# Layer 1's experts in an eight-part transformer kernel: token lists made by products on TensorE, rows gathered and answers scattered tile by tile

## The chip, the cores and the metric

The kernel runs on one core of a Trainium2 chip. The metric is the device time of one execution in microseconds. The engines of the core run their own instruction streams and meet through semaphores: PE (TensorE, matrix products), DVE (VectorE), ACT (ScalarE), POOL (GpSimd) and SP (SyncE), which here only issues transfers. POOL can also issue transfers whose rows are picked by a list of indices (indirect DMA).

## The reference, cut to what matters

Four layers, each a cross-attention followed by a token-mixing part and a feed-forward part. `B * S` is 2 * 512 = 1024 tokens of width 128. The change concerns the feed-forward part of layer 1 alone, where each token goes to the one expert of eight with the largest logit:

```
logits = xf @ Wg.T
idx = jnp.argmax(logits, axis=-1)
for e in range(E):                      # E = 8
    m = (idx == e)[:, None]
    h = relu(xf @ W1[e] + b1[e])        # 128 -> 512
    out = out + m * (h @ W2[e] + b2[e]) # 512 -> 128
```

## The kernel before

The 1024 tokens lie in on-chip memory as eight tiles of 128 (NT = 8); `r_res` holds them, token t * 128 + p in partition p. The kernel sorts the tokens by expert so that each expert multiplies only its own. Each expert's queue is padded to whole tiles of 128 rows, so 8 + 8 - 1 = 15 tiles (`TILES1`) always suffice, each with one expert.

`places1` on DVE (line 1794) and PE (line 2439) works out where each token goes: a mask of the chosen expert, a product with a triangle of ones to count the tokens ahead, the first tile of each expert, and from these `slot_i`, the row of each token in the sorted order (line 1820). Then `tile_e`, the expert of each tile (line 1827). After that DVE runs `centre_weights` (lines 1365 to 1369), which prepares layer 2's weights and has nothing to do with the experts, and `add_biases` (line 1862).

The rows take a path through HBM. POOL (`queues1`, line 890) scatters the eight token tiles into `queued`, one indirect DMA each, `sent` counting them. SP loads tile by tile from `queued` into four buffers `D["xin"]` (`tokens`, line 722) and that tile's expert weights, 514 KB, into four buffers `W0` (`weights`, line 717). It stores each tile's answer into `answers` (line 738). When all 15 are stored, POOL gathers the eight token tiles back out of `answers` with eight indirect DMAs (line 901), and DVE adds them to `r_res` (line 1856).

SP's loop over the tiles is in one order: for tile j it waits for the turned tile j and loads tokens j + 4, waits for output j and loads weights j + 4, waits for answer j and stores it. So tokens j + 5 are issued behind the wait for answer j.

PE's order for the tiles is written out by hand too (line 2446 on). `turned(j)` transposes the tile's tokens, `hidden(j)` multiplies by W1, `output(j)` by W2:

```
turned(0)
turned(1)
hidden(0)
for j in range(TILES1):
    if j + 2 < TILES1:
        turned(j + 2)
    if j + 1 < TILES1:
        hidden(j + 1)
    output(j)
```

DVE copies each turned tile out (`features`, line 1835) and each answer (`answer`, line 1841) into one of four buffers `D["y"]`; ACT applies ReLU (line 1233). Behind the last answer PE runs `prep(2)`, layer 2's keys and values (lines 2033 to 2085), with ACT's copies of its results (lines 993 and 999). DVE, behind the sum of line 1856, runs two layer norms; then layer 2's attention begins with PE's line 2100.

Of the kernel before, what the change touches and what calls it, by code (L numbers as in the profile page):

```python
# [58 lines left out]
E0 = 16  # L59
SLOTS = E0 * CAPACITY  # L60
TILES1 = B * S // P + 8 - 1
assert CAPACITY == P
HS, DS = 16, 8

# [20 lines left out]
def queue_constants():  # L85

    e = np.arange(8)
    wide = lambda v: np.broadcast_to(np.asarray(v, np.float32).reshape(1, -1), (P, np.size(v)))
    return {
        "r_steps": wide(P * e),  # L90
        "r_ahead": wide(P * (e[None, :] < e[:, None])),
        "r_within": wide(e[None, :] <= e[:, None]),
        "r_tile": wide(np.arange(16)),
    }


# [81 lines left out]
    return np.concatenate([w1.reshape(8, 4, P, P).transpose(0, 2, 1, 3).reshape(8, P, 4 * P), w2], 2)  # L178


def program(nc, x, mask, packed, experts, rows, zeros, out, answers, queued, parts_q, parts_k, at):


    ctx = ExitStack()
    with ctx:
        def sb(name, shape, dt=F32):
            return ctx.enter_context(nc.sbuf_tensor(name, shape, dt))
# [28 lines left out]
        pool_pad = sb("pool_pad", [P, 8])  # L216
        n_sum = sb("n_sum", [P, 40])
        slot_i = sb("slot_i", [P, 16], I32)
        tile_e = sb("tile_e", [P, 16], I32)
        s1_now = sb("s1_now", [P, 2, 4])  # L220
        ident_bf = sb("ident_bf", [P, P], BF16)
        later_bf = sb("later_bf", [P, P], BF16)
# [63 lines left out]
        ranks, row_sums = D["xin"][:, 0:P], D["xin"][:, 2 * P:2 * P + 64]  # L286
        chosen = [D["back"][:, n * 1024:(n + 1) * 1024] for n in range(2)]
        W0 = [wexp[:, 0, :], wexp[:, 1, :], D["w"][:, 0:1028], D["w"][:, 1028:2056]]


        in_x, in_mask, stored, const_ok = sems("in_x in_mask stored const_ok")
# [326 lines left out]
        def _(sp):  # L618
# [88 lines left out]
            sp.dma_start(queued, zeros).then_inc(cleared, 16)  # L707
# [7 lines left out]
            def queues1():  # L715

                def weights(j):
                    e = sp.value_load(tile_e[0:1, j:j + 1], min_val=0, max_val=7)
                    src = experts[1].rearrange("e p n -> p e n")[:, bass.ds(e, 1), :]
                    sp.dma_start(W0[j % 4].unsqueeze(1), src).then_inc(w0_in[j % 4], 16)  # L720

                def tokens(j):
                    sp.dma_start(D["xin"][:, j % 4 * P:(j % 4 + 1) * P], queued[j * P:(j + 1) * P, :]).then_inc(q_in[j % 4], 16)

                sp.wait_ge(tiles_ok, 1)
                for j in range(4):
                    weights(j)
                sp.wait_ge(sent, 16 * NT)
                for j in range(4):
                    tokens(j)  # L730
                for j in range(TILES1):
                    if j + 4 < TILES1:
                        sp.wait_ge(d_T, AFTER0 + j + 1)
                        tokens(j + 4)
                        sp.wait_ge(d_O, AFTER0 + j + 1)
                        weights(j + 4)
                    sp.wait_ge(d_y, HELD0 + j + 1)
                    sp.dma_start(answers[j * P:(j + 1) * P, :], D["y"][:, j % 4 * P:(j % 4 + 1) * P]).then_inc(d_stored[j % 4], 16)

            queues1()  # L740
            for l in range(2, 4):
# [23 lines left out]
        def _(pool):  # L765
# [123 lines left out]

            def queues1():  # L890

                pool.wait_ge(cleared, 16)
                pool.wait_ge(m_xn, 2 + B)
                pool.wait_ge(slots_ok, 2)
                for t in range(NT):
                    pool.indirect_dma_start(queued, bass.IndirectOffsetOnAxis(ap=slot_i[:, t:t + 1], axis=0),
                                            r_res[:, t * P:(t + 1) * P], None).then_inc(sent, 16)
                for side in range(4):
                    pool.wait_ge(d_stored[side], STORED0 + 16 * len(range(side, TILES1, 4)))
                for t in range(NT):  # L900
                    pool.indirect_dma_start(D["back"][:, t * P:(t + 1) * P], None, answers,
                                            bass.IndirectOffsetOnAxis(ap=slot_i[:, t:t + 1], axis=0)).then_inc(d_back[t // TB], 16)

            def router_norm3():

# [387 lines left out]
        def _(dve):  # L1293
# [443 lines left out]
            def gating(l):  # L1737
# [53 lines left out]
                if l != 2:  # L1791
                    add_biases(l)

            def places1():
                n, E_ = NT * 8, 8
                shape = [P, NT, E_]
                t3 = lambda v: v[:, 0:n].rearrange("p (t e) -> p t e", e=E_)
                e8 = lambda v: v.rearrange("p (e k) -> p e k", k=8)
                square = [P, 8, 8]
                m, pre, ga = t3(M["m12"]), t3(M["pre"]), t3(M["ga"])  # L1800
                tiles_of, start = small[:, 0, 32:40], small[:, 0, 40:48]
                ended = small[:, 1, 32:40]
# [12 lines left out]
                step.then(dve.tensor_tensor(e8(M["mk"][:, 64:128]), e8(w("r_ahead")), each, ALU.mult))  # L1815
                step.then(dve.tensor_reduce(start, e8(M["mk"][:, 64:128]), AX_X, ALU.add))
                step.then(dve.tensor_tensor(ga, t3(bank(0, 0, n)), start.unsqueeze(1).broadcast_to(shape), ALU.add))
                step.then(dve.tensor_tensor(ga, ga, m, ALU.mult))
                step.then(dve.tensor_reduce(small[:, 0, 48:56], ga, AX_X, ALU.add))
                dve.tensor_scalar(slot_i[:, 0:NT], small[:, 0, 48:56], 1.0, None, ALU.subtract).then_inc(slots_ok, 1)  # L1820
                step.then(dve.tensor_tensor(e8(M["mk"][:, 128:192]), e8(w("r_within")), each, ALU.mult))
                step.then(dve.tensor_reduce(ended, e8(M["mk"][:, 128:192]), AX_X, ALU.add))
                past = M["pre"][:, P:2 * P].rearrange("p (j e) -> p j e", e=8)
                step.then(dve.tensor_tensor(past, ended.unsqueeze(1).broadcast_to([P, 16, 8]),
                                            w("r_tile").unsqueeze(2).broadcast_to([P, 16, 8]), ALU.is_le))
                step.then(dve.tensor_reduce(small[:, 1, 40:56], past, AX_X, ALU.add))
                dve.tensor_scalar(tile_e[:, 0:16], small[:, 1, 40:56], 7.0, None, ALU.min).then_inc(tiles_ok, 1)

            def experts1():

# [6 lines left out]
                def answer(j):  # L1837
                    dve.wait_ge(d_O, AFTER0 + j + 1)
                    if j >= 4:
                        dve.wait_ge(d_stored[j % 4], STORED0 + 16 * (j // 4))  # L1840
                    dve.tensor_copy(D["y"][:, j % 4 * P:(j % 4 + 1) * P], bank(4 + j % 2, 0, P)).then_inc(d_y, 1)

                places1()
                centre_weights()
                dve.wait_ge(sent, 16 * NT)
                add_biases(1)
                features(0)
                features(1)
# [3 lines left out]
                    answer(j)  # L1852
                for b in range(B):
                    r_ = r_res[:, b * S:(b + 1) * S]
                    dve.wait_ge(d_back[b], BACK0 + 16 * TB)
                    step.then(dve.tensor_tensor(r_, r_, D["back"][:, b * S:(b + 1) * S], ALU.add))

            def add_biases(l):
# [150 lines left out]
        def _(pe):  # L2009
# [429 lines left out]
            def places1():  # L2439
# [3 lines left out]
                mm(bank(0, 0, n), w("before"), M["m12"][:, 0:n], start=True, stop=True)  # L2443
                mm(bank(0, 0, n), w("ones"), M["pre"][:, 0:n], start=False, stop=True, skip_group_check=True).then_inc(g_loc, 1)

            def experts1():

                def turned(j):
# [23 lines left out]

                places1()
                turned_gates(1)
                biases(1)
                pe.wait_ge(slots_ok, 2)
                turned(0)
# [158 lines left out]
```

## Time and profile before

| | us |
|---|---|
| median of 3 runs | 1107.84 (1106.42 to 1111.03) |
| the profiled execution | 1109.69 |
| its span in the trace | 1107.9 |
| mean granted clock of PE | 0.876 |

The rows further down are in microseconds from the span's start. A row of the timeline gives the start, the busy time, engine, line, operation, written tile <- read tiles, shape and how many instructions are merged in it; in brackets, how long the engine sat idle before it and who released it. `arena` is the large work buffer that holds `xin`, `xe`, `h`, `y`, `back`, and two of the four weight buffers (`wexp` is the other two). PEclk is the granted clock of TensorE as a share of 2.4 GHz, so that 0.50 is 1.2 GHz.

### The profile page before, as it was taken

The numbers are of one execution on the slowest core, as the hardware profiler recorded it, in microseconds if no ns is written. First come the engines' busy times: TensorE is split into PE (matmuls) and PEld (weight loads), VectorE is DVE, ScalarE is ACT, GpSimd is POOL, SyncE is SP. The second block draws the span as 40 slices with busy tenths as digits, with TensorE's granted clock in tenths as the row PEclk, the third lists the DMA queues.
The fourth block names the chain that finished last, engine by engine and source line by source line (L and its number), as shares of the span: only waits on it lengthen the run. The fifth ranks groups of instructions, "written<-read, shape, count | busy, mean of one in ns | idle before, by whom it ended". The sixth has DMA issues, their size and how long they took to land. (4 is left out here: it accounts for less than half of the span.)

```text
span 1107.9 us, 14863 instructions
## 1 busy us (share of the span) xinstructions
PE 877.4 (79%) x5294; PEld 602.6 (54%) x5294; DVE 577.2 (52%) x1254; ACT 410.1 (37%) x763; POOL 239.3 (22%) x274
## 2 busy tenths in 40 slices
PE   6895989839974654675769688998799988789998
PEld 4673445429962533565359522232466676557776
DVE  5784435446456556117567577771454548522111
ACT  3340535633332200342433326666322234343443
POOL 0543301000043205115545413000000014210110
PEclk9996869959987965796889959999899989978999
DMA  7005230053510001650000224100011100001111
GB/s 319 1 20 124 77 85 24 2 226 88 169 41 8 1 0 47 184 152 15 1 1 2 83 60 130 45 2 1 7 38 43 52 1 1 1 0 31 34 36 35
DMA packets 36031, 60.47 MB, mean 55 GB/s; under 512 B 4016, under 2 KB 27504, under 8 KB 35568
## 3 DMA queue, kind: packets, MB, share of 16 engines
q1 hardware_dynamic: 34944, 57.54, 16.7%
q0 software_dynamic: 1024, 2.10, 0.7%
q8 instruction: 38, 0.62, 0.2%
q14 instruction: 25, 0.20, 0.1%
HBM read 50.06 MB, written 10.35 MB: 55 GB/s over the span
## 5 line engine op out<-in xcount | busy, mean ns | idle before, releaser
L1578 DVE TENSOR_REDUCE arena<-psum 128x2 f32<-128x1024 f32 (+3 forms) x128 | 127.1, 1020 | 81.5 <-PE psum L2250 49.9
L1091 ACT ACTIVATE arena<-psum 128x512 f32<-128x512 f32 (+3 forms) x256 | 115.9, 515 | 87.1 <-PE psum L2263 48.0
L2521 PE MATMUL psum<-xT_all,wexp 128*128 128x512 f32 x272 | 124.6, 603 | 0.9 <-ACT arena L1192 0.6
L2247 PE MATMUL psum<-arena 72*128 72x512 bf16 (+3 forms) x256 | 83.0, 396 | 24.6 <-DMA arena<-parts_q 11.8
L777 POOL TENSOR_TENSOR rstd<-var,held 128x8 f32<-128x8 f32 (+3 forms) x22 | 46.0, 2099 | 252.9 <-DVE var L1333 229.7
L2175 PE MATMUL psum<-values_out_all,arena 128*128 128x128 f32 x560 | 76.4, 284 | 26.6 <-ACT arena L1055 26.0
L852 POOL TENSOR_TENSOR arena<-arena,small 128x616 f32<-128x616 f32 x56 | 68.0, 1217 | 125.7 <-DVE small L1510 125.4
L1917 DVE SCALAR_TENSOR_TENSOR x_res<-psum,arena,x_res 128x128 f32<-128x128 f32 x136 | 38.3, 344 | 101.6 <-PE psum L2536 101.6
L2175 PEld LDWEIGHTS psum<-values_out_all,arena 128*128 128x128 f32 x560 | 67.2, 192 | 36.2 <-ACT arena L1055 35.0
L2260 PE MATMUL psum<-arena 75*128 75x512 bf16 (+3 forms) x256 | 76.2, 362 | 8.2 <-DMA arena<-arena 6.5
L1042 ACT ACTIVATE arena<-arena 128x616 f32<-128x616 f32 x56 | 40.2, 717 | 108.1 <-DVE arena L1506 108.1
L2521 PEld LDWEIGHTS psum<-xT_all,wexp 128*128 128x128 f32 x272 | 50.3, 195 | 53.5 <-issue 48.3
L2247 PEld LDWEIGHTS psum<-arena 72*128 72x128 bf16 x256 | 23.4, 106 | 88.5 <-DVE arena L1578 45.5
L1203 ACT ACTIVATE arena<-psum,wexp,s_now 128x512 f32<-128x512 f32 x64 | 48.2, 778 | 62.3 <-PE psum L2521 59.1
L2536 PEld LDWEIGHTS psum<-arena 128*128 128x128 f32 x512 | 62.2, 199 | 6.9 <-issue 6.9
L2536 PE MATMUL psum<-arena 128*128 128x128 f32 x512 | 62.4, 283 | 0.0
L2301 PE MATMUL psum<-arena 128*32 128x512 f32 (+3 forms) x512 | 61.1, 556 | 1.5 <-ACT arena L1104 1.5
L1502 DVE TENSOR_REDUCE small<-psum 128x8 f32<-128x616 f32 x56 | 44.0, 787 | 34.5 <-PE psum L2152 25.2
L2152 PE MATMUL psum<-keys_of_tokens,xT_all 128*128 128x512 f32 (+1 forms) x160 | 52.3, 453 | 3.9 <-ACT xT_all L962 2.2
L2260 PEld LDWEIGHTS psum<-arena 75*128 75x128 bf16 x256 | 25.8, 104 | 40.4 <-ACT arena L1091 15.1
L1055 ACT ACTIVATE arena<-psum 128x640 f32<-128x640 f32 x56 | 38.8, 692 | 24.0 <-PE psum L2166 24.0
L1506 DVE TENSOR_TENSOR arena<-psum,small 128x616 f32<-128x616 f32 x56 | 44.8, 799 | 1.9
(326 smaller groups left out, 1532.4 us busy)
## 6 DMA issues: line engine op xcount, KB each, us to landing
wexp<-experts SPq DMA_DIRECT2D x24, 514.0 KB, 3.7
arena<-experts SPq DMA_DIRECT2D x15, 514.0 KB, 3.7
parts_k<-wexp SPq DMA_DIRECT2D x12, 384.0 KB, 3.0
arena<-parts_k SPq DMA_DIRECT2D x48, 96.0 KB
arena<-parts_q SPq DMA_DIRECT2D x48, 96.0 KB
arena<-rows SPq DMA_DIRECT2D x8, 512.0 KB, 8.0
wexp<-experts SPq DMA_DIRECT2D x9, 384.0 KB, 3.1
held<-packed SPq DMA_DIRECT2D x1, 2375.0 KB, 15.8
```

The lines of the kernel that those rows point to most:

```text
L777: pool.tensor_tensor(dst, src, half[0:src.shape[0], 0:n], ALU.pow).then_inc(done, 1)
L852: pool.tensor_tensor(e, e, inv, ALU.mult).then_inc(e_mul, 1)
L1091: act.activation(p_self[:, n % 2, kt % 2, j, lo:S], bank(t_bank("keys", c, k), lo, S), ACT.Exp, scale=DS ** -0.5).then_inc(ut_ok, 1)
L1203: act.activation(hT[:, b, c * BANK:(c + 1) * BANK], bank(c, 0, BANK), func, **kw).then_inc(h_ok, 1)
L1578: dve.tensor_reduce(top[:, x % 2, qt, j:j + 2], src, AX_X, ALU.max, negate=True).then_inc(us_ok, 1)
L2152: last = mm(psum[:, first + lo:first + hi], tokens, rows[:, b, half, lo:hi], start=True, stop=True)
L2175: last = mm(bank(sum_bank(l, t), 0, P), PT3[l][:, n % 3, c * P:(c + 1) * P], VW[:, t // TB, half, c * P:(c + 1) * P], start=(half == 0 and ...
L2247: last = mm(bank(first + n, 0, W), q_ring[0:ROWS, x % 4, j + n, qt * P:(qt + 1) * P], k_ring[0:ROWS, x % 4, j + n, 0:W], start=True, stop= ...
L2260: last = mm(bank(first, lo, S), k_ring[0:ROWS + 3, x % 4, j, kt * P:(kt + 1) * P], q_ring[0:ROWS + 3, x % 4, j, lo:S], start=True, stop=True)
L2301: last = mm(psum[32 * j:32 * j + 32, 7 * BANK + lo:8 * BANK], v_wide[b][:, kt, 4 * g + j, :], p_self[:, n // 2 % 2, kt % 2, j, lo:S], star ...
L2521: mm(bank(c, 0, BANK), wexp[:, side, c * P:(c + 1) * P], xT_all[:, b * S:(b + 1) * S], start=True, stop=True).then_inc(h_ps, 1)
L2536: last = mm(bank(4 + b, t * P, (t + 1) * P), hT[:, b, c * BANK + t * P:c * BANK + (t + 1) * P], down, start=(c == 0), stop=(c == C - 1))
```

## The change

The list of tokens is made the other way round: for each of the tiles, which token stands in each row. DVE writes two 0/1-like operands in bf16 (`lane_of`, 128 x 8 x 128, and `place_of`, 128 x 8 x 2 x 24), PE multiplies them in eight products accumulated in one bank (`rows_of_tiles`), and DVE turns the sums into `row_i`, the token number of row p of tile j; a row that no token has gets a number of its own behind the 1024 tokens.

SP stores `r_res` once, in token order, into `tokens_in`. POOL gathers the rows of tile j out of `tokens_in` with the list (`fetch`) and scatters the answer of tile j into `sorted_out` at the same list (`deliver`): for j = 0 to 14 `deliver(j)`, then `fetch(j + 4)`. SP's loop keeps only the weights. When all 15 answers are delivered, SP loads the answers back in token order with two plain loads, one per batch. On PE, `rows_of_tiles` stands ahead of `biases(1)`. `tile_e` gets 24 columns in place of 16.

```diff
+                sp.wait_ge(m_xn, 2 + B)
+                sp.dma_start(tokens_in[0:B * S, :].rearrange("(t p) d -> p t d", p=P),
+                             r_res[:, :].rearrange("p (t d) -> p t d", d=P)).then_inc(sent, 16)
                 sp.wait_ge(tiles_ok, 1)
                 for j in range(4):
                     weights(j)
-                sp.wait_ge(sent, 16 * NT)
-                for j in range(4):
-                    tokens(j)
-                for j in range(TILES1):
-                    if j + 4 < TILES1:
-                        sp.wait_ge(d_T, AFTER0 + j + 1)
-                        tokens(j + 4)
-                        sp.wait_ge(d_O, AFTER0 + j + 1)
-                        weights(j + 4)
-                    sp.wait_ge(d_y, HELD0 + j + 1)
-                    sp.dma_start(answers[j * P:(j + 1) * P, :], D["y"][:, j % 4 * P:(j % 4 + 1) * P]).then_inc(d_stored[j % 4], 16)
+                for j in range(TILES1 - 4):
+                    sp.wait_ge(d_O, AFTER0 + j + 1)
+                    weights(j + 4)
+                for side in range(4):
+                    sp.wait_ge(d_back[side], BACK0 + 16 * len(range(side, TILES1, 4)))
+                for b in range(B):
+                    sp.dma_start(D["back"][:, b * S:(b + 1) * S].rearrange("p (t d) -> p t d", d=P),
+                                 sorted_out[b * S:(b + 1) * S, :].rearrange("(t p) d -> p t d", p=P)).then_inc(d_stored[b], 16)
...
+                def fetch(j):
+                    if j >= 4:
+                        pool.wait_ge(d_T, AFTER0 + j - 3)
+                    pool.indirect_dma_start(D["xin"][:, j % 4 * P:(j % 4 + 1) * P], None, tokens_in,
+                                            bass.IndirectOffsetOnAxis(ap=row_i[:, j:j + 1], axis=0)).then_inc(q_in[j % 4], 16)
+
+                def deliver(j):
+                    pool.wait_ge(d_y, HELD0 + j + 1)
+                    pool.indirect_dma_start(sorted_out, bass.IndirectOffsetOnAxis(ap=row_i[:, j:j + 1], axis=0),
+                                            D["y"][:, j % 4 * P:(j % 4 + 1) * P], None).then_inc(d_back[j % 4], 16)
...
                 pool.wait_ge(cleared, 16)
-                pool.wait_ge(m_xn, 2 + B)
+                pool.wait_ge(sent, 16)
                 pool.wait_ge(slots_ok, 2)
-                for t in range(NT):
-                    pool.indirect_dma_start(queued, bass.IndirectOffsetOnAxis(ap=slot_i[:, t:t + 1], axis=0),
-                                            r_res[:, t * P:(t + 1) * P], None).then_inc(sent, 16)
-                for side in range(4):
-                    pool.wait_ge(d_stored[side], STORED0 + 16 * len(range(side, TILES1, 4)))
-                for t in range(NT):
-                    pool.indirect_dma_start(D["back"][:, t * P:(t + 1) * P], None, answers,
-                                            bass.IndirectOffsetOnAxis(ap=slot_i[:, t:t + 1], axis=0)).then_inc(d_back[t // TB], 16)
+                for j in range(4):
+                    fetch(j)
+                for j in range(TILES1):
+                    deliver(j)
+                    if j + 4 < TILES1:
+                        fetch(j + 4)
...
+            def places_in_tiles(n):
+
+                at, first = Z["at"][:, 0:n], Z["first"][:, 0:n]
+                slot = small[:, 0, 48:48 + n]
+                whole, lane = slot_i[:, 0:n], lane_i[:, 0:n]
+                step.then(dve.tensor_scalar(whole, slot, 1.0, None, ALU.subtract))
+                step.then(dve.tensor_scalar(lane, whole, P - 1, None, ALU.bitwise_and))
+                step.then(dve.tensor_tensor(first, whole, lane, ALU.subtract))
+                step.then(dve.tensor_scalar(at, lane, 1.0, None, ALU.add))
+                wide_j = [P, n, 24]
+                which = place_of[:, 0:n]
+                step.then(dve.tensor_tensor(which[:, :, 1, :], first.unsqueeze(2).broadcast_to(wide_j),
+                                            w("r_first").unsqueeze(1).broadcast_to(wide_j), ALU.is_equal))
+                dve.tensor_scalar(which[:, :, 0, :], which[:, :, 1, :], w("r_lane"), None, ALU.mult)
+                step.then(dve.tensor_tensor(which[:, :, 1, :], which[:, :, 1, :],
+                                            w("r_block", 0, n).unsqueeze(2).broadcast_to(wide_j), ALU.mult))
+                dve.tensor_tensor(lane_of[:, 0:n, :], at.unsqueeze(2).broadcast_to([P, n, P]),
+                                  w("places").unsqueeze(1).broadcast_to([P, n, P]), ALU.is_equal).then_inc(g_m, 1)
...
-                dve.tensor_scalar(slot_i[:, 0:NT], small[:, 0, 48:56], 1.0, None, ALU.subtract).then_inc(slots_ok, 1)
+                places_in_tiles(NT)
+                dve.wait_ge(g_loc, 3)
+                off, row = Z["off"], Z["row"]
+                lanes, blocks = bank(1, 0, 24), bank(1, 24, 48)
+                step.then(dve.scalar_tensor_tensor(off, blocks, 0.0, w("r_unused"), ALU.is_equal, ALU.mult))
+                step.then(dve.tensor_scalar(row, blocks, float(P), -float(P), ALU.mult, ALU.add))
+                step.then(dve.tensor_tensor(row, row, lanes, ALU.add))
+                dve.tensor_tensor(row_i[:, 0:24], row, off, ALU.add).then_inc(slots_ok, 1)
...
                     if j >= 4:
-                        dve.wait_ge(d_stored[j % 4], STORED0 + 16 * (j // 4))
+                        dve.wait_ge(d_back[j % 4], BACK0 + 16 * (j // 4))
...
-                dve.wait_ge(sent, 16 * NT)
+                dve.wait_ge(sent, 16)
...
-                    dve.wait_ge(d_back[b], BACK0 + 16 * TB)
+                    dve.wait_ge(d_stored[b], STORED0 + 16)
...
+            def rows_of_tiles(n):
+
+                pe.wait_ge(g_m, 3)
+                for i in range(n):
+                    last = mm(bank(1, 0, 48), lane_of[:, i, :], place_of[:, i].rearrange("p k j -> p (k j)"),
+                              start=(i == 0), stop=(i == n - 1))
+                last.then_inc(g_loc, 1)
```

## Rows read from the trace of the kernel before

**Rows 1.** Busy time by stage: the tiles' loop, and what follows until the sum.

```profile
451.00:491.00 40.00, 33.20 (x255) 30.62 (x256) 8.38 (x30) 17.15 (x60) 0.00 (x0) 0.95 0.66 188
491.00:507.00 16.00, 12.84 (x61) 10.56 (x59) 1.50 (x3) 6.41 (x10) 7.63 (x8) 0.79 0.14 38
```

**Rows 2.** Timeline from the places to the first tile, DVE, PE, POOL and SP.

```profile
432.96 0.55 PEld L2443 LDWEIGHTS psum<-arena,held 128*128 128x128 f32 x2
...
435.95 0.17 DVE L1820 TENSOR_SCALAR slot_i<-small 128x8 int32<-128x8 f32 x1
...
436.54 0.29 DVE L1824 TENSOR_TENSOR arena<-small,held 128x128 f32<-128x128 f32 x1
...
436.96 1.07 POOL L896 DMA_INDIRECT queued<-r_res,slot_i  x1 [9.60 <-DVE slot_i L1820]
437.18 0.17 DVE L1827 TENSOR_SCALAR tile_e<-small 128x16 int32<-128x16 f32 x1
...
438.39 1.48 SPq L720 DMA_DIRECT2D wexp<-experts  x2
...
446.33 0.96 POOL L896 DMA_INDIRECT queued<-r_res,slot_i  x1 [0.30 <-issue]
...
448.59 1.22 DVE L1862 TENSOR_TENSOR r_res<-r_res,psum 128x1024 f32<-128x1024 f32 x1 [5.80 <-DMA queued<-r_res,slot_i]
...
450.99 0.72 DVE L1835 COPY arena<-psum 128x128 f32<-128x128 f32 x2 [1.17 <-PE psum L2452]
```

**Rows 3.** Timeline of the tiles' loop: answers 0, 1, 4 and 14, tokens 6.

```profile
456.04 0.29 DVE L1841 COPY arena<-psum 128x128 f32<-128x128 f32 x1 [2.03 <-PE psum L2469]
...
457.93 0.29 DVE L1841 COPY arena<-psum 128x128 f32<-128x128 f32 x1 [1.41 <-PE psum L2469]
...
459.76 0.43 SPq L723 DMA_DIRECT2D arena<-queued  x1
...
463.24 0.33 PE L2452 MATMUL psum<-held,arena 128*128 128x128 f32 x1 [0.43 <-DMA arena<-queued]
...
465.40 0.29 DVE L1841 COPY arena<-psum 128x128 f32<-128x128 f32 x1 [1.50 <-PE psum L2469]
...
490.25 0.29 DVE L1841 COPY arena<-psum 128x128 f32<-128x128 f32 x1 [1.29 <-PE psum L2469]
```

**Rows 4.** DMA issues: KB each, median us from issue to landing.

```profile
wexp<-experts SPq DMA_DIRECT2D x24, 514.0 KB, 3.7
...
arena<-queued SPq DMA_DIRECT2D x15, 64.0 KB, 3.4
...
out<-x_res SPq DMA_DIRECT2D x1, 512.0 KB, 3.2
...
arena<-answers,slot_i POOLq DMA_INDIRECT x24, 2.5
queued<-r_res,slot_i POOLq DMA_INDIRECT x8, 3.6
```

**Rows 5.** Timeline behind the last answer: gathers, sum, layer 2's first products.

```profile
494.65 0.99 POOL L901 DMA_INDIRECT arena<-answers,slot_i  x1 [47.36 <-DMA answers<-arena]
...
506.17 0.69 DVE L1856 TENSOR_TENSOR r_res<-r_res,arena 128x512 f32<-128x512 f32 x1 [4.48 <-DMA arena<-answers,slot_i]
...
511.76 0.70 ACT L999 ACTIVATE values_out_all<-psum 128x640 f32<-128x640 f32 x1 [0.26 <-PE psum L2085]
...
522.84 2.31 PE L2100 MATMUL psum<-held,arena 77*128 77x77 f32 x16 [11.12 <-DVE arena L1441]
```

**Rows 6.** Busy time and clock in and behind three idle spells of PE.

```profile
496.40:499.50 3.10, 0.00 (x0) 0.00 (x0) 0.00 (x0) 3.08 (x6) 2.41 (x3) 0.93 0.20 57
499.50:506.00 6.50, 6.46 (x27) 6.46 (x28) 0.71 (x1) 1.29 (x2) 3.78 (x4) 0.51 0.19 50
558.50:560.80 2.30, 0.00 (x1) 0.00 (x0) 2.23 (x3) 1.20 (x1) 1.79 (x2) 0.93 0.00 0
355.35:357.40 2.05, 0.00 (x0) 0.00 (x0) 2.02 (x4) 1.31 (x2) 0.83 (x2) 1.00 0.00 0
```

More of the change, by code:

```diff
@@ L61 @@
 TILES1 = B * S // P + 8 - 1
+ROWS_OUT = B * S + TILES1 * P
 assert CAPACITY == P
@@ L92, in queue_constants @@
         "r_within": wide(e[None, :] <= e[:, None]),
-        "r_tile": wide(np.arange(16)),
+        "r_tile": wide(np.arange(24)),
+        "r_first": wide(P * np.arange(24)),
+        "r_block": wide(np.arange(1, 17)),
+        "r_lane": np.arange(P, dtype=np.float32).reshape(-1, 1),
+        "r_unused": B * S + P + np.arange(24 * P, dtype=np.float32).reshape(24, P).T,
     }
@@ L178, in row_layout, with program @@
     return np.concatenate([w1.reshape(8, 4, P, P).transpose(0, 2, 1, 3).reshape(8, P, 4 * P), w2], 2)
-def program(nc, x, mask, packed, experts, rows, zeros, out, answers, queued, parts_q, parts_k, at):
+def program(nc, x, mask, packed, experts, rows, zeros, out, answers, sorted_out, tokens_in, parts_q, parts_k, at):
     ctx = ExitStack()
@@ L218, in program @@
         slot_i = sb("slot_i", [P, 16], I32)
-        tile_e = sb("tile_e", [P, 16], I32)
+        tile_e = sb("tile_e", [P, 24], I32)
+        row_i = sb("row_i", [P, 24], I32)
+        lane_i = sb("lane_i", [P, 16], I32)
         s1_now = sb("s1_now", [P, 2, 4])
@@ L288, in program @@
         W0 = [wexp[:, 0, :], wexp[:, 1, :], D["w"][:, 0:1028], D["w"][:, 1028:2056]]
+        Z = take(dict(lane=1024, which=2 * 24 * 8, off=24, row=24, at=16, first=16))
+        lane_of = Z["lane"].bitcast(BF16).rearrange("p (n c) -> p n c", c=P)
+        place_of = Z["which"].bitcast(BF16).rearrange("p (n k j) -> p n k j", k=2, j=24)
         in_x, in_mask, stored, const_ok = sems("in_x in_mask stored const_ok")
@@ L706, in _ @@
                 sp.dma_start(rows3[:, e, :], rows[e]).then_inc(n_in, 16)
-            sp.dma_start(queued, zeros).then_inc(cleared, 16)
+            sp.dma_start(tokens_in[B * S:ROWS_OUT, :], zeros).then_inc(cleared, 16)
             with sp.Fori(0, E0 // 4 - 1) as i:
@@ L720, in weights @@
                     sp.dma_start(W0[j % 4].unsqueeze(1), src).then_inc(w0_in[j % 4], 16)
-                def tokens(j):
-                    sp.dma_start(D["xin"][:, j % 4 * P:(j % 4 + 1) * P], queued[j * P:(j + 1) * P, :]).then_inc(q_in[j % 4], 16)
+                sp.wait_ge(m_xn, 2 + B)
+                sp.dma_start(tokens_in[0:B * S, :].rearrange("(t p) d -> p t d", p=P),
+                             r_res[:, :].rearrange("p (t d) -> p t d", d=P)).then_inc(sent, 16)
                 sp.wait_ge(tiles_ok, 1)
@@ L1819, in places1 @@
                 step.then(dve.tensor_reduce(small[:, 0, 48:56], ga, AX_X, ALU.add))
-                dve.tensor_scalar(slot_i[:, 0:NT], small[:, 0, 48:56], 1.0, None, ALU.subtract).then_inc(slots_ok, 1)
+                places_in_tiles(NT)
[6 more added lines that the diff above has]
+                dve.tensor_tensor(row_i[:, 0:24], row, off, ALU.add).then_inc(slots_ok, 1)
                 step.then(dve.tensor_tensor(e8(M["mk"][:, 128:192]), e8(w("r_within")), each, ALU.mult))
                 step.then(dve.tensor_reduce(ended, e8(M["mk"][:, 128:192]), AX_X, ALU.add))
[L1823 to L1827, printed above, removed]
+                past = M["h"][:, 2048:2240].rearrange("p (j e) -> p j e", e=8)
+                step.then(dve.tensor_tensor(past, ended.unsqueeze(1).broadcast_to([P, 24, 8]),
+                                            w("r_tile").unsqueeze(2).broadcast_to([P, 24, 8]), ALU.is_le))
+                step.then(dve.tensor_reduce(small[:, 2, 0:24], past, AX_X, ALU.add))
+                dve.tensor_scalar(tile_e[:, 0:24], small[:, 2, 0:24], 7.0, None, ALU.min).then_inc(tiles_ok, 1)
             def experts1():
@@ L2474, in experts1 @@
                 turned_gates(1)
+                rows_of_tiles(NT)
                 biases(1)
@@ L2628 @@
     answers = nc.dram_tensor("answers", (SLOTS, P), F32, kind="Internal").ap()
-    queued = nc.dram_tensor("queued", (TILES1 * P, P), F32, kind="Internal").ap()
+    sorted_out = nc.dram_tensor("sorted_out", (ROWS_OUT, P), F32, kind="Internal").ap()
+    tokens_in = nc.dram_tensor("tokens_in", (ROWS_OUT, P), F32, kind="Internal").ap()
     parts_q = nc.dram_tensor("parts_q", (2, B, 3 * P, S), BF16, kind="Internal").ap()
@@ L2632 @@
     program(nc, ap["x"], ap["mask"], ap["packed"], [ap[f"experts{l}"] for l in range(4)], ap["rows"], ap["zeros"], out, answers,
-            queued, parts_q, parts_k, at)
+            sorted_out, tokens_in, parts_q, parts_k, at)
     r = run_bass_kernel_spmd(nc, [arrays], core_ids=[0])
```

## The prediction

> **What bounds the kernel now.** I read the busy time by stage first [rows 1]. In the tiles' loop, 451 to 491, PE is busy for 33.2 of 40 us at a clock of 0.95: near its limit, not at it. From 491 to 507 PE and ACT work on layer 2's keys, and DVE, which layer 1 needs, is busy for 1.5 of 16 us: a wait. So three pieces count: from the places to the first tile, the loop, and from the last answer to the sum.
>
> The timeline ahead of the loop [rows 2] shows DVE's list of places at 435.95, POOL's eight scatters from 436.96 to 446.33 and DVE idle for 5.80 us until they have landed at 448.59. The first features are copied at 450.99, because the tokens are loaded only then. What is to be seen: the scatters end last here, and `centre_weights`, from the end of 437.18 to 5.80 us before 448.59, some 5.4 us, costs nothing.
>
> In the loop [rows 3] answers 0 and 14 start 34.21 us apart, 2.44 a tile. Follow one round: answer 1 ends at 458.22, SP stores it and issues tokens 6 at 459.76, they land 3.4 to 3.5 us later [rows 3, 4], PE turns them at 463.24, and answer 4 ends at 465.69. This wait comes around once for **three** tiles, 7.47 us, since tokens j + 5 stand behind the store of answer j, and PE turns tile j + 5 ahead of output j + 3. From the turn to the end of that answer are 2.45 us.
>
> Behind the loop [rows 5]: answer 14 ends at 490.54, the gathers start at 494.65, the last half of the sum starts at 506.17, 15.63 us after the answer.
>
> **The change part by part: the start.** DVE gets four small instructions at 0.20 each (0.17 for 128x8 [rows 2] and the gap to the next), 0.80; three over 192 elements, put at 0.39 each with the gap: 0.29 for 128 elements [rows 2], 0.07 more for 64 more, 1.17; one over 1024 elements, 1.22 as the one at 448.59. That is 3.2, to 439.15. PE's eight bf16 products don't occur here: the nearest rows are fp32 products at the same low clock, 0.27 a load [rows 2], which is the upper bound, 2.2 us for eight; half of it is the lower, 1.1. As bf16 makes one pass, I take 1.3, to 440.45. Four small DVE instructions more, 0.9: `row_i` is ready at 441.3, where `slot_i` was at 436.12. The fetches start as late after it as the scatters did, 0.84, so at 442.15, and land 2.5 later [rows 4]: nothing waits for them. `tile_e` comes 5.3 later, at 442.65, the weights are issued 1.04 behind it as before [rows 2], at 443.7, and land by 447.5 (3.7 [rows 4]). The cover of `centre_weights` is gone: DVE ends it at 448.1, `add_biases` at 449.35, and copies the first features then, 1.65 earlier than at 450.99. So DVE's own work ends last, and eight scatters buy **1.65 us**; with the bounds of the products 0.7 to 1.9. Answer 0 ends at 454.7. The store of `r_res` (512 KB, 3.2 us for the same size [rows 4]) is issued before 432.96, where PE already counts tokens, and is over long before 442; the four weight loads behind it on SP's queue are not held. PE's biases run a few us later, ahead of 448.
>
> **The loop.** The tokens now wait on POOL: `deliver(j)` for answer j, behind it `fetch(j + 4)`. PE turns tile j + 4 ahead of output j + 2. The round closes after **two** tiles, not three. Its parts: from DVE's end to an indirect DMA's start 0.84 [rows 2]; the scatter's issue, (446.33 - 436.96) / 7 = 1.34 at worst and 1.27 where DVE is quiet (0.96 and the 0.30 of issue), I take 1.27; the gather's landing; 2.45 from the turn to the answer. The landing is 2.5 alone, 3.6 beside four weight loads (median of the scatters [rows 4]), 2.2 at the least (446.33 to 448.55). The weights of tile j + 4 are issued some 0.4 after answer j and the gather 2.1, mostly behind them, so 2.8. A round is 0.84 + 1.27 + 2.8 + 2.45 = 7.36, that is 3.68 a tile. Turned tiles 4 to 14 let answers 2 to 12 go, six rounds, 44.2; answers 13 and 14 need none, and end 3.9 later as before. The loop lasts 48.1 in place of 34.2: **+13.9**. POOL itself needs 2.54 a tile, above the 2.44 of before, so that even with no latency this loop isn't shorter.
>
> The Trainium skill (DMA: Bandwidth & Descriptors, Anatomy of one DMA, the gpsimd path) gives an indirect DMA about 2.0 us plus its bytes over 436 GB/s, 2.15 for 64 KB. By it a round would be 6.7 and the sum 3.9 lower; the rows of the gathers, 2.5, stand nearer to this case.
>
> **The clock.** In a round PE works for twice some 2.1 us and then sits idle for about as long as the gather takes, 2.5 to 3.6. Before, it waited 0.43 in the row shown [rows 3]. In this trace the clock fell in a spell of 3.1 and in one of 2.3, and not in one of 2.05 [rows 6]; behind the first it stayed at 0.51 for 6.5 us of work. At 1.2 GHz the products of a turn, a hidden and an output take about twice as long, and 2.45 becomes 4.0. When it falls, PE works almost without a break and it rises again; I take half of the 1.55 in each of six rounds: **+4.5**, bounds 0 and 9.3.
>
> **The end.** Answer 14, 0.84 to the last scatter, 2.5 until it lands (2.2 to 3.6), SP's load at once; 256 KB in 2.8, between the 2.5 of 64 KB gathered and the 3.2 of 512 KB [rows 4]; 0.5 for the second load. The last half of the sum starts 6.9 us after answer 14, where it was 15.63: **-8.7** (bounds -9.5 and -7). Eight gathers in a row become two loads. Behind it layer 2's first product (522.84) stood 16.67 after the sum and ACT's last copy of prep (511.76 to 512.46) 21.9 after answer 14 [rows 5]; now the first would be due 23.6 after answer 14: prep stays hidden, by 1.7 us.
>
> **Sum.** -1.65 + 13.9 + 4.5 - 8.7 = +8.05 us. The profiled execution of before took 1109.69, with 1.8 around its span of 1107.9; it would be 1117.7. It lies 1.85 above the median, so that the median goes to 1115.9. The measurement tells 0.5%, 5.5 us, from no change.
>
> **Rivals.**
> *The clock holds.* PE's idle spells stay between the 2.05 and 2.3 us of the rows, or the work on either side keeps it up. Then +3.5, 1111.4: no measurable change. For it speaks that the spell with 2.05 passed; against it that every gather in the trace takes 2.5.
> *The clock falls in every round.* For it speaks the spell of 2.3 us. All of 1.55 is paid six times: +12.8, 1120.6. The Trainium skill (TensorE: Matmul & The Clock Gate, HAM oscillation) describes this case, short bursts of products with a wait for a DMA between them, and has every burst start cold; by it this rival, not the half, is the sum. The rows show both kinds of spell, so it gets no more than its share below.
> *The gather is as slow as the scatters beside the weights*, 3.6 or more: 0.8 in six rounds, +4.8 on the sum, 1120.7. Against it: four loads stood in line there, here one.
> *Faster.* POOL's wake decides: between two indirect DMAs in a row it takes 0.30 [rows 2], not 0.84. If `deliver`, the only thing POOL waits to do, starts so soon, and the gather lands in 2.2, a round is 0.30 + 1.27 + 2.2 + 2.45 = 6.2 and the loop 41.2. With a clock that holds the sum is -1.65 + 7.0 - 9.5 = -4.2, 1103.7. A round has to be below 6.0 us for it to be measurable; the one wake from a wait in the trace, 0.84, speaks against it.
>
> **How the numbers follow.** Half-cold clock, round about 7.4 (+5.5 to +11): 0.40. Clock holds (0 to +5.5): 0.33. Cold in each round, or the slow gather (+11 to +17): 0.20. Faster by over 5.5: 0.07. The first and third are slower by over 0.5%, but for the lower edge of the first, 0.04: slower 0.56, same 0.37, faster 0.07. Range: 1106.5 (the clock holds, gather 2.2, a short wake in part) to 1123 (cold in each round and 3.0 of landing); about a tenth is left out on either side.
>
> **What will show it.** `row_i` near 441.3 and features 0 near 449.4, with DVE busy without a gap from 436 on, not waiting for a DMA. Answers in pairs, two every 7.4 us, PE waiting for the gathers of `fetch` in front of each pair, answer 14 near 507 to 508. PEclk in the loop well under the 0.95 of before. From answer 14 to the last half of the sum about 7. Wrong would make it: answers evenly under 3 us apart (the round isn't the bound), a PEclk of 1.00 there, or the weights of `tile_e` landing later than DVE's 448.

## The result

| | before | after |
|---|---|---|
| median | 1108.74 us of 4 runs (1106.42 to 1111.03) | 1123.48 us of 4 runs (1120.02 to 1124.14) |
| the profiled execution, its span | 1109.69, 1107.9 | 1123.24, 1121.4 |

The ratio is 1.0145, with a 95% interval of 1.0118 to 1.0172: **slower by 1.45%**, some 15 us, where 0.7% and 8 us were forecast. The time lies 0.5 us above the range that was given.

Start of layer 1's experts after the change, from the timeline (start, busy time, engine, line, what, how many; in brackets the idle time before it). These answer to [rows 2].

```profile
438.75 0.50 PE L2492 MATMUL psum<-arena 128*128 128x48 bf16 x8 [3.20 <-DVE arena L1826]
...
439.94 0.18 DVE L1862 TENSOR_TENSOR row_i<-arena 128x24 int32<-128x24 f32 x1
...
440.92 1.04 POOL L902 DMA_INDIRECT arena<-tokens_in,row_i  x1 [13.82 <-DVE row_i L1862]
...
446.96 1.22 DVE L1904 TENSOR_TENSOR r_res<-r_res,psum 128x1024 f32<-128x1024 f32 x1
448.21 0.49 DVE L1877 COPY arena<-psum 128x128 f32<-128x128 f32 x2
```

The list is ready at 440.12; DVE has no gap from there to the first features at 448.21, and waits for no DMA, where before it stood idle for 5.80 us. The first features come 2.78 earlier than the 450.99 of before. But answer 0 ends at 454.65, only 1.68 earlier: from the features to the answer, 6.44 in place of 5.34, PE works at half clock for longer (0.50 until 454.6; before it was 1.00 from 455.0). Of both gains 0.27 isn't the change's: in this execution `slot_i` itself starts at 435.68, before at 435.95.

One round of the loop after the change, answers 6 to 8, from the timelines of DVE, PE, POOL and SP. It answers to [rows 3].

```profile
482.37 0.29 DVE L1883 COPY arena<-psum 128x128 f32<-128x128 f32 x1 [2.94 <-PE psum L2519]
...
482.94 0.99 POOL L907 DMA_INDIRECT sorted_out<-arena,row_i  x1 [5.10 <-DVE arena L1883]
483.07 2.25 SPq L730 DMA_DIRECT2D arena<-experts  x2
...
484.23 0.97 POOL L902 DMA_INDIRECT arena<-tokens_in,row_i  x1 [0.30 <-issue]
...
484.27 0.29 DVE L1883 COPY arena<-psum 128x128 f32<-128x128 f32 x1 [1.41 <-PE psum L2519]
...
488.69 0.39 PE L2502 MATMUL psum<-held,arena 128*128 128x128 f32 x1 [4.46 <-DMA arena<-tokens_in,row_i]
488.87 1.94 PE L2510 MATMUL psum<-arena,wexp 128*128 128x128 f32 x8
...
492.48 0.29 DVE L1883 COPY arena<-psum 128x128 f32<-128x128 f32 x1 [3.07 <-PE psum L2519]
```

To be seen: answers in pairs, 482.37 and 484.27, the next pair from 492.48. Answer 6 ends at 482.66; 0.28 later POOL issues its scatter, 1.29 later the gather of tile 10, which lands 4.46 after its issue; PE, idle for those 4.46 us, turns it at 488.69; answer 8 ends 4.08 later, at 492.77. SP's two weight loads of the pair are issued at 483.07 and 484.99, on either side of that gather. A round of two tiles, 10.11 us. The six rounds take 9.17, 8.91, 9.93, 10.11, 10.44 and 7.93, and answers 0 to 14 span 60.67 us where it was 34.21.

Busy time by stretch (length, then PE, PEld, DVE, ACT and POOL busy with their counts, granted clock, DMA share, GB/s): the loop from answer 0 to 14, the end until the last half of the sum, and one idle spell of PE with the stretch behind it.

```profile
454.65:515.32 60.67, 36.25 (x227) 34.73 (x226) 7.04 (x26) 14.86 (x52) 24.50 (x25) 0.83 0.43 122
515.32:521.65 6.33, 5.73 (x24) 3.30 (x24) 0.70 (x2) 2.39 (x3) 0.97 (x1) 1.00 0.34 104
484.40:488.60 4.20, 0.00 (x0) 0.00 (x0) 0.16 (x1) 0.20 (x1) 2.76 (x3) 1.00 0.83 254
488.60:491.60 3.00, 2.91 (x14) 2.91 (x15) 0.29 (x1) 0.67 (x3) 0.00 (x0) 0.54 0.16 56
```

The clock is 1.00 while PE is idle, 0.54 for the first tile behind it, and rises during the second (0.89 from 491.60 to 494.40). DMA is 0.83 busy in the very stretch in which the gather is awaited. The last half of the sum starts 6.33 us after answer 14, where it was 15.63.

Issues of two of the new transfers in the DMA view (KB, median from issue to landing), which answer to [rows 4]:

```profile
arena<-sorted_out SPq DMA_DIRECT2D x2, 256.0 KB, 2.9
...
arena<-tokens_in,row_i POOLq DMA_INDIRECT x15, 3.7
```

Where the time went: answer 0 earlier by 1.68, the loop longer by 26.46, the end shorter by 9.30, which puts the last half of the sum 15.48 later (521.65 against 506.17). The addition into `x_res` behind it is 15.50 later (532.19 against 516.69); layer 2's first sum of attention is 13.88 later (600.84 against 586.96), and so it stays until the end, 13.5. Layer 2's start gives the 1.6 back at a higher clock: in the 5.5 us from 555.0 the granted clock is 1.00, where in the same work of before, from 539.5, it was 0.69, and four instructions of 512 columns there take 1.89 in place of 3.10.

### The profile page after: what moved, and what is told of

It is laid out like the page before. It is cut to its first block and busy times, and to the rows that moved or that the text cites. A ratio compares the mean times of both kernels' runs of the same rounds, so it can differ in the third digit from the quotient of the medians.

```text
span 1121.4 us, 14872 instructions
## 1 busy us (share of the span) xinstructions
PE 887.1 (79%) x5297; PEld 612.7 (55%) x5302; DVE 580.7 (52%) x1265; ACT 410.2 (37%) x763; POOL 253.4 (23%) x288
```

## The experiments

Each is the changed kernel with the edit shown; "..." stands for lines left out. Loop means from the end of answer 0 to the end of answer 14; landing is read for the six gathers that let a round go (tiles 4, 6, ... 14), from issue to PE's turn. The runs with few or half of the weights, without scatters and with extra products are one execution each, so their times tell only large differences; the argument rests on the rows of their traces.

### Why the gather takes 4.1 us: the weights, or the scatter ahead of it

The six landings in the changed kernel were 4.25, 3.59, 4.32, 4.46, 4.89 and 3.25, mean 4.13, against 2.5 in [rows 4]. First, from tile 4 on, only 64 of the 1028 columns of the weights are loaded:

```diff
                     sp.wait_ge(d_O, AFTER0 + j + 1)
-                    weights(j + 4)
+                    weights(j + 4, 964)      # columns 964 to 1027 alone
```

> The changed kernel, but from tile 4 on only the last 64 of the 1028 weight columns of each tile are loaded (32 KB in place of 514 KB), so those tiles are multiplied with weights left over from other tiles. It asks why a gather in the loop takes about 4.1 us from issue to landing (six rounds: 3.2 to 4.9) and not the 2.5 of before. Theory A, the gather shares the DMA engines with two weight loads of 514 KB that SP issues in the same moment: the landing falls to 2.5 to 2.8, a round of two tiles from 9.4 to about 7.5, answer 0 to answer 14 from 60.7 to about 49 us, the span by about 11. Theory B, the gather stands behind the scatter of the answer that POOL issued 1.3 us ahead of it on the same queue: the landing stays near 4, the span stays within 2 us.

Timeline of a round, answers 2 to 4:

```profile
459.63 0.29 DVE L1883 COPY arena<-psum 128x128 f32<-128x128 f32 x1 [1.50 <-PE psum L2519]
...
461.50 0.97 POOL L902 DMA_INDIRECT arena<-tokens_in,row_i  x1 [0.30 <-issue]
...
464.08 0.33 PE L2502 MATMUL psum<-held,arena 128*128 128x128 f32 x1 [1.83 <-DMA arena<-tokens_in,row_i]
...
466.24 0.29 DVE L1883 COPY arena<-psum 128x128 f32<-128x128 f32 x1 [1.50 <-PE psum L2519]
```

Here 459.63 is answer 2 and 466.24 answer 4. The gather of tile 6 lands 2.58 after its issue; the six lie between 2.54 and 2.64, mean 2.59 (of the five gathers of odd tiles four do too, within 0.03, and that of tile 9 took 3.73, for which the trace shows no reason). A round is 6.6 us, the loop 43.04, the clock in it 1.00, the time 1104.7 of one run, 18.8 under the changed kernel. Theory A holds, and by more than was expected of it, because with the short waits the clock doesn't fall either. The edit takes away both, so the loop's 17.6 us are not the weights' price alone; the landing, 1.5 a round, is read by itself. The round is the sum of its parts: 0.28 + 1.30 + 2.58 + 2.45 = 6.61.

The counter-test takes the scatters out. SP stores each answer as a plain block in tile order, so that the answers don't come back in token order:

```diff
+                    sp.wait_ge(d_y, HELD0 + j + 1)
+                    sp.dma_start(sorted_out[j * P:(j + 1) * P, :], D["y"][:, j % 4 * P:(j % 4 + 1) * P]).then_inc(d_stored[j % 4], 16)
...
-                for j in range(TILES1):
-                    deliver(j)
-                    if j + 4 < TILES1:
-                        fetch(j + 4)
+                for j in range(TILES1 - 4):
+                    pool.wait_ge(d_y, HELD0 + j + 1)
+                    fetch(j + 4)
```

> The changed kernel with the scatters taken out: SP stores each answer as one plain block in tile order (so the answers are not brought into token order), POOL still waits for answer j and then gathers tile j + 4. Theory A (weights beside the gather): the landing stays near 4, a round is 0.28 + 4.1 + 3.7 = 8.1, the loop about 52. Theory B (behind the scatter): the landing falls to 2.5 to 2.8, the round to about 6.7, the loop about 44.

The six landings were 4.11, 4.27, 4.10, 5.70, 4.46 and 4.35, no shorter than with the scatters; the loop took 50.58, with the 1.3 us of issue gone from each round and a clock of 0.90 (1112.29 us). So a scatter ahead on POOL's queue isn't what makes the gather late. SP's stores move the same 64 KB in its place, so this run doesn't say what those bytes cost beside the gather.

Between the two, half of the weights' columns (the edit of the first run with column 514):

> The changed kernel, but from tile 4 on only the last 514 of the 1028 weight columns are loaded (257 KB in place of 514 KB; the rest is left over from other tiles). The landing of the gathers in the loop was 2.6 us with 32 KB and 4.1 with 514 KB. Theory, it is the bytes that stand in the DMA engines ahead of and beside the gather: something between, 3.2 to 3.5, a round of about 7.3 to 7.8 with the clock holding for part of it, loop 47 to 50. Rival, any pair of full-width loads costs the whole 1.5 us however short: landing near 4, loop above 55.

The landings were 3.03, 2.63, 2.85, 2.60, 3.19 and 2.50, mean 2.80 (1109.9 us): half of the bytes cost 0.2 us and the other half 1.3. The expectation of 3.2 to 3.5 missed. The loop of 48.10 came out as expected for another reason: the clock was 0.86, so that turn to answer took 3.1 in place of 2.45. In these three runs the delay isn't proportional to the bytes; how it grows was not measured further.

### What the clock costs

Products that nobody reads are put in front of the awaited turn, so that PE does not sit idle:

```diff
+                pe.wait_ge(b2_ok, 2)
                 for j in range(TILES1):
+                    if j >= 2 and j % 2 == 0 and j + 2 < TILES1:
+                        for k in range(7):                       # 4 in the second run
+                            mm(bank(7, 0, BANK), w("ones"), xT_all[:, 0:BANK], start=True, stop=True)
                     if j + 2 < TILES1:
                         turned(j + 2)
```

> The changed kernel with seven extra products of 512 columns (3.0 us at full clock) in PE's stream ahead of the turns of tiles 4, 6, 8, 10, 12 and 14, into a bank that nobody reads. Theory: the fallen clock costs 0.5 us of each round over what was forecast and 1.3 over a clock that holds (turn to answer 3.7 in place of 2.45). Then the granted clock in the loop goes from 0.83 to 0.95 or more, turn to answer to about 2.5, the round from 9.4 to about 8.2, the span shrinks by 6 to 8 us. Rival: the clock is a symptom and costs nothing, because the wait for the gather takes up what PE gains: the span stays within 2 us.

Inconclusive. I had put the products at half their price (each call is two instructions of 0.44 in the trace): PE was busy for 61.70 of 62.45 us, the clock was 1.00, and the turns now waited for the extra products and not for the gathers (loop 62.45, time 1128.44). So again with four:

> The changed kernel with four extra products per round of two tiles where the run before had seven. Those took about 0.86 us each at full clock (not 0.43), 6 us for seven, and held up the turn themselves; four take 3.4 us, less than the 4.1 for which PE waits. Theory: the clock stays at 1.00 once it is up, turn to answer is 2.4 in place of 3.7, a round 0.28 + 1.30 + 4.1 + 2.4 = 8.1 in place of 9.4, six rounds 8 us less: loop about 53, span about 1114. Rival, the clock costs nothing: loop stays at 59 to 61.

```profile
474.39 3.60 PE L2535 MATMUL psum<-xT_all,held 128*128 128x512 f32 x8
474.56 0.97 POOL L902 DMA_INDIRECT arena<-tokens_in,row_i  x1 [0.30 <-issue]
...
479.01 0.33 PE L2502 MATMUL psum<-held,arena 128*128 128x128 f32 x1 [1.02 <-DMA arena<-tokens_in,row_i]
```

The extra work ends 1.0 us before the gather lands, 4.45 after its issue (0.65 to 1.02 in the first five rounds; in the sixth PE did not wait for the gather); turn to answer is 2.4, the clock 1.00, the loop 52.01 and the time 1114.85 of one run. Four more products per round make the loop **8.7 us shorter**, with the gathers landing no sooner (4.09 to 4.45). That is the price of the clock in the changed kernel: 7.8 in the six rounds, 1.3 each, and 0.8 in the last two tiles.

### Undoing the round

The two calls of POOL's loop change places, and in a second kernel the gather goes one tile further ahead:

```diff
+                fetch(4)                       # the second kernel only
                 for j in range(TILES1):
-                    deliver(j)
-                    if j + 4 < TILES1:
-                        fetch(j + 4)
+                    if j + 4 < TILES1:         # j + 5 in the second kernel
+                        fetch(j + 4)           # j + 5
+                    deliver(j)
```

> The changed kernel with the two calls of POOL's loop in the other order: for each j first the gather of tile j + 4, then the scatter of answer j. Theory, the round closes after two tiles because the gather stands behind the wait for answer j: now it stands behind answer j - 1 and the round closes after three tiles, (0.3 + 1.3 + 4.1 + 2.5 to 3.7) / 3 = 2.7 to 3.1 us a tile, the loop takes 38 to 44 in place of 60.7, the time falls by 17 to 23 us to 1101 to 1107: below the changed kernel and about at, or just below, the kernel before. Rival, POOL's 2.6 us of issuing per tile or the engines of the DMA are the limit and not the round: the loop stays above 50.

> The changed kernel with the gather of tile j + 5 ahead of the scatter of answer j, so that the round closes after four tiles. Theory of rounds: (0.3 + 1.3 + 4.4 + 2.5) / 4 = 2.1 us a tile is now less than POOL's own 2.57 us of issuing for the two indirect DMAs of a tile, which becomes the limit: loop about 36 to 38, no more than 2 us below the 37.65 of the run with the gather one ahead. Rival, the rounds were still the limit there: loop near 32.

One ahead: loop 37.65, clock 0.95, 1103.65 us median of ten runs, ratio to before 0.995 (0.9925 to 0.9974). Nothing was removed and nothing added against the changed kernel; 23 us of its loop went with the order of two calls, although the gathers land no sooner (median 4.5).

Two ahead: loop 33.85, clock 1.00, 1096.36 us, ratio 0.9887 (0.9856 to 0.9919). The loop lost 3.8 us against one ahead, where at most 2 was expected because POOL's issuing would be the limit. From the timeline:

```profile
460.44 0.97 POOL L902 DMA_INDIRECT arena<-tokens_in,row_i  x1 [0.30 <-issue]
...
460.94 1.16 PE L2511 MATMUL psum<-arena,wexp 128*128 128x128 f32 x8 [0.95 <-DMA wexp<-experts]
```

POOL issues without a gap, 2.57 a tile, from 453.99 to 477.15, but PE has its tokens in hand: its nine waits for a DMA in the loop, 4.1 us in all, are for weights. So POOL's issuing is full and still isn't shown to be the limit; the loop takes 2.42 a tile. One ahead, PE waited six times for tokens, 8.1 us in all.

### One half of the change at a time

Tokens the old way, answers the new way. DVE makes the list behind `slot_i` and `tile_e`, while the scatters run:

```diff
+                def tokens(j):
+                    sp.dma_start(D["xin"][:, j % 4 * P:(j % 4 + 1) * P], tokens_in[j * P:(j + 1) * P, :]).then_inc(q_in[j % 4], 16)
...
+                sp.wait_ge(sent, 16 * NT)
+                for j in range(4):
+                    tokens(j)
                 for j in range(TILES1 - 4):
+                    sp.wait_ge(d_T, AFTER0 + j + 1)
+                    tokens(j + 4)
                     sp.wait_ge(d_O, AFTER0 + j + 1)
                     weights(j + 4)
...
-                for j in range(4):
-                    fetch(j)
+                for t in range(NT):
+                    pool.indirect_dma_start(tokens_in, bass.IndirectOffsetOnAxis(ap=slot_i[:, t:t + 1], axis=0),
+                                            r_res[:, t * P:(t + 1) * P], None).then_inc(sent, 16)
+                pool.wait_ge(slots_ok, 3)
                 for j in range(TILES1):
                     deliver(j)
-                    if j + 4 < TILES1:
-                        fetch(j + 4)
```

> One half of the change: the tokens go the old way (eight scatters into a queue, plain loads of SP), the answers the new way (a scatter per tile, two plain loads at the end). The list row_i is made behind slot_i and tile_e, while the scatters run, and SP no longer waits for answers. Theory (the end of the change gains 9 us, its loop alone loses): start as in the kernel before, loop 30 to 34 us (before 34.2), last answer to sum 6.3 to 7 in place of 15.6: 9 to 12 us below the kernel before, 1096 to 1099. Rival, POOL's scatters beside the loads slow the loop as the gathers do: loop 38 or more, time within 0.5% of before.

1096.84 us median of six, ratio 0.990 (0.9872 to 0.9928). Answer 0 ends at 456.67 (before 456.33); the loop takes 34.33 (34.21) and the end 6.45 (15.63). Of the three pieces only the end gains: the last half of the sum comes 8.7 us earlier, of the 10.1 by which this span is shorter.

Tokens the new way, with no answer awaited in front of a gather, answers the old way:

```diff
+                    sp.wait_ge(d_y, HELD0 + j + 1)
+                    sp.dma_start(answers[j * P:(j + 1) * P, :], D["y"][:, j % 4 * P:(j % 4 + 1) * P]).then_inc(d_stored[j % 4], 16)
...
-                for j in range(TILES1):
-                    deliver(j)
-                    if j + 4 < TILES1:
-                        fetch(j + 4)
+                for j in range(TILES1 - 4):
+                    fetch(j + 4)
+                for side in range(4):
+                    pool.wait_ge(d_stored[side], STORED0 + 16 * len(range(side, TILES1, 4)))
+                for t in range(NT):
+                    pool.indirect_dma_start(D["back"][:, t * P:(t + 1) * P], None, answers,
+                                            bass.IndirectOffsetOnAxis(ap=slot_i[:, t:t + 1], axis=0)).then_inc(d_back[t // TB], 16)
```

> The other half: tokens stored once and gathered tile by tile by the list, with no wait for an answer in front of a gather; the answers go the old way (SP stores each, eight gathers at the end). Theory: start 1.7 us earlier as in the changed kernel, loop 31 to 35, end 15.6: the time 1 to 5 us below the kernel before. Rival, the gather by itself is too slow beside the weight loads (4.1 to 4.5 us) even where it is issued early: loop above 40 and slower than before.

1104.22 us median of ten, ratio 0.9978 (0.9958 to 0.9998): loop 34.92, end 13.78, gathers landing in 4.7 in the median. A gather that takes 4.7 costs the loop next to nothing when it is issued early: 0.7 us over the 34.21 of before, and no wait of PE for tokens in it. Answer 0 ends at 453.27, 3.1 sooner, but `slot_i` stood 1.53 earlier in this execution, so that the start gains half of it. The end is 1.85 shorter, where no gain was expected; why was not looked into. The whole is 0.2%, hardly clear of no change.

### A version that beats both

The gather two ahead once more, and beside it the same kernel with `centre_weights` in five pieces behind answers 3 to 7:

```diff
-                centre_weights()
+                pieces_left = centre_weights()     # now yields between its instructions
...
                     answer(j)
+                    if 3 <= j < 8:
+                        next(pieces_left)
```

> The kernel with the gather of tile j + 5 ahead of the scatter of answer j once more, beside the next one on the same chip: 1095 to 1098, 1% below the kernel before.

> The same, and centre_weights (5.5 us of DVE, needed only by layer 2's preparation) cut into five pieces behind answers 3 to 7 instead of ahead of the first tile. Theory, DVE's own work is what ends last ahead of the first tile, the first gather having landed 4.5 us before: the first features are copied about 4 us earlier, where the first weights (issued 5 us behind) become the limit, answer 0 comes 1.5 to 2.5 us earlier, the time is 1.5 to 2.5 us less. Rival, the pieces delay DVE's copies in the loop as much: no difference.

The first: 1097.40 us, ratio 0.9911 (0.9887 to 0.9934). The second: 1095.39 us, ratio 0.9895 (0.987 to 0.9921). The medians differ by 2.0, with intervals that overlap; the traces agree with it: answer 0 ends at 451.84, not 454.60, the loop takes 33.53 and 33.51, and the last half of the sum starts at 491.77, not 494.47, while the list was only 0.28 earlier. The pieces cost DVE's copies nothing that shows.

## Why the prediction went wrong

The way was right: the start gains little, the end gains much, and the loop loses more than both because its round closes after two tiles. The sizes of two terms were wrong, in the same direction.

**The start.** Forecast -1.65, measured -1.68, and the agreement is luck. The features came 1.1 earlier than forecast, 0.8 of it because the products took 0.50 and not 1.3, and 0.27 because `slot_i` stood earlier in this execution. PE's first tile took 1.1 longer, because the clock rose only in the second, where before it was up for output 0. Without the 0.27 the start gained 1.4.

**The end.** Forecast -8.7, measured -9.3. The parts of the forecast, 0.84 + 2.5 + 2.8 + 0.5, add up to 6.6 and not to the 6.9 that was used. Measured are 0.28 to the last scatter (515.60), 2.39 until SP issues its loads (517.99), 2.79 to the first half of the sum (520.78) and 0.87 to the second, 6.33 in all: half of the 0.6 is that slip, and half the short wake less what the second load took.

**The loop.** Forecast +13.9 and +4.5 for the clock, 18.4; measured +26.5. By the parts of a round, means of six:

| | forecast | measured |
|---|---|---|
| answer to scatter (wake of POOL) | 0.84 | 0.28 |
| issue of the scatter | 1.27 | 1.30 |
| landing of the gather | 2.8 | 4.13 |
| turn to answer | 2.45 + 0.75 | 3.71 |
| a round | 8.1 | 9.42 |

**The step that failed is the landing of the gather.** It was put at 2.8, "mostly behind" the weights. The trace had the price: the scatters beside four weight loads took 3.6 in the median [rows 4], and this was made a rival with the argument that one load stood in line, not four. But answers come in pairs, and SP issues two loads, one ahead of the gather and one behind it (483.07 and 484.99 around 484.23); in the 4.2 us in which the gather is awaited the DMA engines are 0.83 busy. This term alone is 8.0 us over six rounds. The run with few weights shows that it is the weights (2.59), the run without scatters that it isn't a scatter ahead on POOL's queue (4.10 to 5.70).

**The clock** was rightly seen as a cost, at 4.5 us, half of a fully cold round; it was 7.6 by turn to answer, and 8.7 by the run with four extra products. It was treated as a chance of its own, apart from the landing: with landings of 2.59 it held at 1.00 in every round, with 4.13 it fell in every round. The two rivals, "the clock falls in every round" at 1120.6 and "the gather is as slow as the scatters" at 1120.7, each came true and came together, and the text had them as alternatives; together they would have been near 1125, less what the wake gave.

The landing doesn't decide it alone, nor does the length of PE's idle spell. Without scatters, tile 4 was turned behind a landing of 4.11 and a spell of 2.55, and the clock stayed at 1.00 through that tile, as behind the next spells of 0.6 to 2.2. With half of the weights, tile 8 was turned behind a landing of 2.85 and a spell of 1.92, with the clock at 1.00 ahead of it, and it fell to 0.50 a microsecond later:

```profile
461.48 0.33 PE L2504 MATMUL psum<-held,arena 128*128 128x128 f32 x1 [2.55 <-DMA arena<-tokens_in,row_i]
```

```profile
471.18 0.33 PE L2502 MATMUL psum<-held,arena 128*128 128x128 f32 x1 [1.92 <-DMA arena<-tokens_in,row_i]
```

So the prediction's sorting of spells by length (2.05 held, 2.3 fell) doesn't carry over to these runs, and what decides stays open. The rule of the Trainium skill (TensorE: Matmul & The Clock Gate, HAM oscillation) by which each burst behind a wait for a DMA starts cold was right for the changed kernel, 0.54 behind the spell shown, and did not hold for the same loop with PE's spells of 0.5 to 2.4 us (1.00). By the fit of the Trainium skill (DMA: Bandwidth & Descriptors, Anatomy of one DMA, the gpsimd path), an estimate of 2.15 us, the landing would have been missed by more; the run nearest to it, with 32 KB of weights, has 2.59.

**The wake of POOL** was too dear by 0.56, 3.4 us over six rounds in the other direction. The 0.84 of [rows 2] is that of POOL's first indirect DMA in layer 1; the first gather of the changed kernel has it too (0.80 behind `row_i`), and the scatters behind it have 0.28, the first of them also, after 8.77 us of idling. In the run with the answers alone the first scatter, behind eight of another loop, has 0.76. What makes a first one dear is not shown.

So +8.0 and +3.1 for landing and clock, -3.4 for the wake and +0.2 for the issue: some 7.8 us beyond the forecast of the loop's six rounds, 0.3 more for the last two tiles. That is the whole distance between 8.05 and the 15.48 at the sum, with the end 0.6 better. The time missed the range by 0.5 us, and it was that close only because the short wake hid 3.4 of the 11.1 us that landing and clock were short.

## What to carry to other kernels

Count the tiles around which a wait closes before pricing what is in it: write down which tile's result the wait stands behind, and which tile's work waits for the transfer. Here the same instructions cost 15 us or won 11, by whether the gather of tile j + 4 stood behind answer j or ahead of answer j - 1.

Price a transfer by a row in which the same neighbours are in flight, not by one where it is alone, and price the clock after the waits, not beside them.

## What the runs showed of the hardware

- A 64 KB indirect gather of 128 rows: 2.54 to 2.64 us from issue to PE's turn with 32 KB loads beside it (six gathers; one of the others took 3.73), 2.80 in the mean with 257 KB loads, 4.13 with 514 KB loads. I had not expected the last step to be so much larger than the first.
- An indirect DMA of the changed kernel's loop that POOL waits to issue starts 0.28 us after the copy that it waits for; the first of layer 1 started 0.80 and 0.84 us after the list was ready. Issued back to back in the loop they start 1.27 to 1.30 us apart.
- PE's clock stayed at 1.00 through an idle spell of 4.2 us and was 0.54 in the 3.0 us of work behind it. With spells of 0.5 to 1.9 us (the first 2.4) and a round of 6.6 it never fell in 43 us. In other runs it held behind a spell of 2.55 and fell behind spells of 1.92 and 2.01: the length of the spell alone doesn't tell.
